# A windowed-attention network in one software pipeline: value products in 16 tiles, two normalizations on GpSimd, and the stages in another order

## The reference, cut to what matters

```python
xn  = layernorm(x) * g1 + b1                      # over the 48 channels
xw  = 7x7 windows of roll(xn, -shift)             # 64 windows of N = 49 tokens per image
q, k, v = split(xw @ qkv_w + qkv_b)               # 6 heads of D = 8 channels
attn = softmax(q*D**-0.5 @ k.T + bias[head] + mask[window])
x  = x + roll(window_reverse((attn @ v) @ proj_w + proj_b), shift)
x  = x + gelu((layernorm(x) * g2 + b2) @ fc1_w + fc1_b) @ fc2_w + fc2_b
```

## Time and profile before

| | |
|---|---|
| median of 3 runs | 5848.9 us (5840.44 to 5856.62) |
| profiled execution | 5841.79 us, its span 5840.0 us |
| busy share of the span | PE 96%, PEld 66%, DVE 83%, ACT 69%, POOL 49% |
| mean granted PE clock | 0.96 of full speed |
| DMA | 11.9% of 16 engines in the queue of the main part |

### The profile page before, as it was taken

How to read it: one execution, slowest core, us unless ns; L and a number is a source line. 1 busy time by engine, 2 the same in 40 slices (tenths; PEclk the granted TensorE clock), 3 DMA queues, 4 the chain that set the end, 5 groups by cost and what they waited for, 6 DMA issues and landing times.

```text
span 5840.0 us, 273732 instructions
## 1 busy us (share of the span) xinstructions
PE 5586.6 (96%) x114818; PEld 3833.3 (66%) x114818; DVE 4841.7 (83%) x7753; ACT 4010.4 (69%) x6155; POOL 2875.1 (49%) x2457
## 2 busy tenths in 40 slices
PE   6799999999999999999999999999999999999987
PEld 3566666666666666666666666666666666666655
DVE  6688888888888888888888788888887888888864
ACT  0277777777777777777777677777776777777760
POOL 4355545555555555554545455555554554455530
PEclk7699999999999999999999999999999999999985
DMA  7311111111111111111111111111111111111118
GB/s 231 97 28 27 30 25 30 28 29 28 28 29 27 30 27 27 30 27 28 30 27 29 26 30 27 29 28 30 27 29 26 29 28 27 28 27 30 28 40 266
DMA packets 288522, 240.35 MB, mean 41 GB/s; under 512 B 43576, under 2 KB 282906, under 8 KB 287002
## 3 DMA queue, kind: packets, MB, share of 16 engines
q1 hardware_dynamic: 246802, 179.90, 11.9%
q0 software_dynamic: 8192, 22.49, 1.2%
q10 hardware_dynamic: 32282, 20.03, 1.1%
HBM read 112.93 MB, written 109.36 MB: 38 GB/s over the span
## 4 chain that ended last, share of the span: by engine, by line
PE 93%; DMA 3%; issue 3%; DVE 1%; ACTq 0%; ACT 0%; SPq 0%; POOL 0%; DVEq 0%
PE pB L1076 10%; PE pS L1100 10%; PE pS L1088 10%; PE pS L1064 9%; PE pA L1110 6%; PE pA L1152 5%; PE pA L1076 5%; PE pB L1052 5%; PE pS L1076 5%; PE pS L1006 4%; PE pS L1037 4%; PE pB L1131 4%; PE pS L1014 3%; PE pA L1014 3%; PE pA L1142 3%
## 5 line engine op out<-in xcount | busy, mean ns | idle before, releaser
L463 POOL TENSOR_TENSOR S<-S,mx 113x588 f32<-113x588 f32 x1536 | 1803.5, 1185 | 1183.0 <-DVE mx L775 1182.8
L449 POOL TENSOR_TENSOR Kbd<-KT,headmask 128x588 f32<-128x588 f32 x768 | 1018.5, 1326 | 1476.1 <-DVE KT L784 1468.7
L762 DVE TENSOR_TENSOR S<-pS,bias 113x588 f32<-113x588 f32 x1536 | 1145.3, 767 | 357.8 <-PE pS L1064 344.6
L775 DVE TENSOR_REDUCE mx<-S 113x12 f32<-113x588 f32 x1536 | 1126.9, 754 | 0.0
L520 ACT ACTIVATE sq<-pS 112x392 f32<-112x392 f32 x768 | 378.4, 493 | 518.5 <-PE pS L1006 518.2
L1076 PE MATMUL pB<-ident,S 113*113 113x113 f32 x4608 | 651.7, 278 | 0.1
L1100 PE MATMUL pS<-E,keyones 113*32 113x392 f32 x4608 | 626.6, 517 | 26.2 <-issue 26.2
L1076 PEld LDWEIGHTS pB<-ident,S 113*113 113x113 f32 x4608 | 519.1, 180 | 196.1 <-issue 196.1
L1088 PE MATMUL pS<-E,V 113*32 113x98 f32 x18432 | 597.3, 249 | 0.0
L1064 PE MATMUL pS<-Kbd,Qt 24*49 24x147 f32 x24576 | 585.8, 294 | 6.9 <-issue 2.9
L1064 PEld LDWEIGHTS pS<-Kbd,Qt 24*49 24x49 f32 x24576 | 372.5, 118 | 307.9 <-issue 266.4
(11 more groups left out here) (133 smaller groups left out, 9329.7 us busy)
## 6 DMA issues: line engine op xcount, KB each, us to landing
xin<-xT SPq DMA_DIRECT2D x384, 98.0 KB, 2.1
xT<-xout SPq DMA_DIRECT2D x384, 98.0 KB, 1.9
xin<-xT SPq DMA_DIRECT2D x384, 73.5 KB, 2.6
xT<-xout SPq DMA_DIRECT2D x384, 73.5 KB, 1.9
xT<-cm POOLq DMA_DIRECT2D x128, 171.5 KB, 4.0
cm<-xT SPq DMA_DIRECT2D x128, 171.5 KB, 3.5
tm<-in_x SPq DMA_DIRECT2D x128, 147.0 KB
out<-tm ACTq DMA_DIRECT2D x128, 147.0 KB
```

The source lines that it names most:

```text
L449: return pool.tensor_tensor(y, x, m, ALU.mult)
L463: pool.tensor_tensor(s, s, m, ALU.subtract).then_inc(sub_done[half][wh], 1)
L762: dve.tensor_tensor(strided(S[:, b, w, 0, 0, 0:1], [[KEYS, 2], [2 * KEYS, 2 * HP], [1, N]]), strided(pS[0:M2, 2 * wh, 0:1], [[512, 2], [N, ...
L775: dve.tensor_reduce(m, s, AX.X, ALU.max).then_inc(mx_done[half][wh], 1)
```

## The change

1. `value`: one product now gives all 48 value columns of one window (both head halves), and the window half chooses the partitions: windows 0 to 3 come out at partitions 0 to 48, windows 4 to 7 at 64 to 112. 4 x 2 x 2 = 16 products in place of 32. `evac_v` reads each window half for itself, so a head half takes two copies of 192 elements in place of one of 384.
2. `normal1` and `normal2` are issued by POOL and not by DVE, with the same operands.
3. The order of the stages on PE, ACT, DVE, POOL and SP, and the homes in PSUM. `add_bias`, `maxima`, `less_maximum` and `exponentials` remain in their four units. `up`, `hidden_c`, `hidden_ab` and `down_ab`, for instance, now work on s4 where they worked on s5.

```diff
-        HOME = dict(ctr1=0, var1=1, qk=1, value=3, attend=0, sums=1, project=2, ctr2=0, var2=2, up=3, upc=2, down=2, turn00=3, turn01=1, turn10=2, turn11=3)
+        HOME = dict(ctr1=3, var1=3, qk=1, value=2, attend=3, sums=2, project=0, ctr2=0, var2=2, up=2, upc=0, down=1, turn00=2, turn01=3, turn10=3, turn11=1)
...
 # value(j), PE
-                for w in range(P):
+                for k in range(J):
                     for i in range(2):
                         r = HI * i
-                        x = strided(xn1[r:r + C, w, 0, 0:1], [[1, N]])
-                        for hh in range(2):
-                            last = mm(to[HI * hh:HI * hh + N, i, HC * w:HC * (w + 1)], x,
-                                      wv[r:r + C, t, HC * hh:HC * (hh + 1)], start=True, stop=True)
+                        for wh in range(2):
+                            x = strided(xn1[r:r + C, J * wh + k, 0, 0:1], [[1, N]])
+                            last = mm(strided(to[HI * wh:HI * wh + N, i, HC * k:HC * k + 1], [[J * HC, 2], [1, HC]]), x,
+                                      wv[r:r + C, t, :].rearrange("p (a n) -> p a n", a=2), start=True, stop=True)
...
 # evac_v(j, hh), DVE
-                src = strided(home("value")[r:r + N, 0, 0:1], [[512, 2], [D, P * HP], [1, D]])
-                dst = strided(V[r:r + N, j.mod(4), 0, 0, o:o + 1], [[2 * D, 2], [VW, P * HP], [1, D]])
-                return dve.tensor_copy(dst, src)
+                for wh in range(2):
+                    at = HI * wh
+                    src = strided(home("value")[at:at + N, 0, J * HC * hh:J * HC * hh + 1], [[512, 2], [D, J * HP], [1, D]])
+                    dst = strided(V[r:r + N, j.mod(4), J * wh, 0, o:o + 1], [[2 * D, 2], [VW, J * HP], [1, D]])
+                    last = dve.tensor_copy(dst, src)
+                return last
...
 # normal1 and normal2: the same bodies, moved from the DVE block to the POOL block
-                dve.wait_ge(rs1_done, gv(j, 1, 1))
+                pool.wait_ge(rs1_done, gv(j, 1, 1))
...
-                dve.tensor_tensor(xn2[:, :], x1[:, j.mod(2)].rearrange("p r c -> p (r c)"), rs2[:, :], ALU.mult)\
+                pool.tensor_tensor(xn2[:, :], x1[:, j.mod(2)].rearrange("p r c -> p (r c)"), rs2[:, :], ALU.mult)\
...
 # SP
-                if s5:
-                    store(s5)
+                if s4:
+                    store(s4)
...
-            LATEST = [(0, 0)]
+            LATEST = [(1, 0)]
```

More of the change, by code:

```diff
@@ L612, in iteration @@
                     inverse_sums(s3)
[L613 to L616, removed]
+                if s4:
+                    hidden_c(s4)
+                if s4:
+                    hidden_ab(s4)
+                    normal_table()
             sweep(act, iteration)
@@ L878, in iteration @@
             def iteration(s0, s1, s2, s3, s4, s5, s6):
+                if s0:
+                    evac_k(s0)
+                if s0:
+                    evac_q(s0)
+                if s0:
+                    evac_va(s0)
+                if s3:
+                    residual1(s3)
+                if s0:
+                    evac_vb(s0)
                 if s4:
-                    normal_o(s4)
+                    residual2(s4)
                 if s1:
-                    evac_k(s1)
+                    maxima(s1, 1, 1)
                 if s1:
-                    evac_q(s1)
-                if s4:
-                    residual1(s4)
-                if s2:
[L888 to L906, removed]
-                if s0:
[L908 to L912, removed]
+                    maxima(s1, 1, 0)
+                if s0:
+                    add_bias(s0, 0, 0)
+                if s0:
+                    add_bias(s0, 0, 1)
+                if s0:
+                    maxima(s0, 0, 0)
+                if s0:
+                    add_bias(s0, 1, 0)
+                if s0:
+                    add_bias(s0, 1, 1)
+                if s2:
+                    normal_o(s2)
+                if s0:
+                    maxima(s0, 0, 1)
             sweep(dve, iteration)
@@ L1243, in iteration @@
                     elif s4:
-                        pe.wait_ge(lo_done, gv(s4, 1, 1))
-                    var1(s0)
-                if s4:
-                    if s2:
-                        pe.wait_ge(bias_done[1][0], gv(s2, 1, 1))
+                        pe.wait_ge(oT_done, gv(s4, 1, 1))
+                    elif s1:
+                        pe.wait_ge(va1_done, gv(s1, 1, 1))
+                    turn_scores(s3, 1, 0)
+                if s4:
+                    if s3:
+                        pe.wait_ge(exp_done[0][0], gv(s3, 1, 1))
+                    elif s1:
+                        pe.wait_ge(v_done, gv(s1, 1, 1))
+                    elif s5:
+                        pe.wait_ge(hAB_done, gv(s5, 1, 1))
+                    elif s4:
+                        pe.wait_ge(lo_done, gv(s4, 1, 1))
+                    var2(s4)
+                if s1:
+                    if s4:
+                        pe.wait_ge(sq2_done, gv(s4, 1, 1))
+                    elif s5:
+                        pe.wait_ge(hC_done, gv(s5, 1, 1))
+                    elif s2:
+                        pe.wait_ge(bias_done[1][0], gv(s2, 1, 1))
+                    if s3:
+                        pe.wait_ge(exp_done[1][1], gv(s3, 1, 1))
+                    elif s5:
+                        pe.wait_ge(x2_done, gv(s5, 1, 1))
+                    elif s1:
+                        pe.wait_ge(q_done, gv(s1, 1, 1))
+                    elif s2:
+                        pe.wait_ge(bias_done[1][1], gv(s2, 1, 1))
+                    ready()
+                    scores(s1, 0)
+                if s0:
+                    if s3:
+                        pe.wait_ge(exp_done[1][0], gv(s3, 1, 1))
                     elif s0:
@@ L1333, in iteration @@
-                if s3:
+                    sums(s3)
+                if s1:
                     if s1:
@@ L1356, in iteration @@
                     elif s1:
-                        pe.wait_ge(bias_done[0][1], gv(s1, 1, 1))
-                    elif s0:
-                        pe.wait_ge(va1_done, gv(s0, 1, 1))
-                    query_key(s0)
+                        pe.wait_ge(v_done, gv(s1, 1, 1))
+                    value(s0)
+                if s3:
+                    if s4:
+                        pe.wait_ge(hC_done, gv(s4, 1, 1))
+                    elif s1:
+                        pe.wait_ge(bias_done[1][0], gv(s1, 1, 1))
+                    project(s3)
+                if s4:
+                    if s0:
+                        pe.wait_ge(q_done, gv(s0, 1, 1))
+                    elif s1:
+                        pe.wait_ge(bias_done[1][1], gv(s1, 1, 1))
+                    elif s3:
+                        pe.wait_ge(exp_done[1][1], gv(s3, 1, 1))
+                    elif s5:
+                        pe.wait_ge(x2_done, gv(s5, 1, 1))
+                    down_ab(s4)
             sweep(pe, iteration)
```

309 lines of the change are left out of this document (126 added, 183 removed).

## The result

The changed kernel takes 5480.1 us in the median of 4 runs (5476.99 to 5482.14), against 5845.5 of before beside it: ratio 0.9372, 95% interval 0.9356 to 0.9388. That is 365 us, twice the forecast gain, and outside the stated range. The profiled execution took 5478.5 us, its span 5476.5.

What follows compares the result with a forecast made beforehand. PE's stages in sequence, 13.59 us per iteration, were taken as the bound. 5841.8 - 77 (iteration) - 63 (stalls) - 40 (slow clock) = 5662, as median 5669 us; own range 5600 to 5720, 8 in 10 5595 to 5800.

Steps and rivals of the forecast that it cites:

- The value products: PE's `value` stage: 16 products of 48 columns in place of 32, 0.35 us less per iteration (0.20 if dearer).
- The order on PE: PE's stages in new order, at the earlier chain's prices: about 0.13 us dearer per iteration.
- The stalls and the clock: PE's issue stalls at `value` and `sums`: 63 of 84 us go; of the slow clock's 78 us, 40 go.
- density: PE stalls where it uses up its instruction list faster than it is brought; spreading dense stages removes 63 us.
- The normalizations on POOL: `normal1` and `normal2` on POOL: 0.8 us for 392 elements, about 1.2 for the shifted `normal1`; hidden, cost 0.
- The copies: DVE's copies of V before the first transpose: 0.35 us each with 192 elements fewer, done 0.2 us early.
- rival 2: A DVE chain up to the first transposes takes PE's place, PE stands 0.4 us per iteration: 5925 us; chance 0.11.

Runs made afterwards that it cites:

- short logarithm: Against the kernel before, `log_sums` takes the logarithm of only the first quarter of the columns from the second step on: 5731.7 us, ratio 0.9834.

## Why the prediction was wrong

- *The value products*: right. Priced at 0.35 less (0.36 + 0.16 = 0.52 in the chain), measured 0.51 in the chain and 0.34 less by the kernel with the old products.
- *The order on PE*: here it failed, and this is the larger part of the miss: 141 of the 185 us by which the forecast gain of 180 fell short (218 - 77 for the iteration; the stalls and the clock gave 140 - 103 = 37 more). The prediction took 0.78 + 0.74 + 0.74 for three transposes in a row, reading 0.74 in the earlier trace rows as what a second transpose costs, and said that "stage follows stage without a wait for another engine". 0.15 of it was a wait for `lo_done` (the run with the short logarithm shows it), which the chain books as the transpose's own time. The own price is 0.59, and the term was taken twice in the new order, where that wait stands in neither place: 0.30. Both `scores` took 0.68 where 0.74 and 0.70 were taken: 0.08 more; why have one at 0.74 was not tested. `down_ab` took 0.67 for 0.65. 13.37 - 0.30 - 0.08 + 0.02 = 13.01, the measured spacing of the chain. So the rest of the change was not a cost of 0.13 but a gain of 0.23 beside the products' 0.34, and the 77 us for both became 218.
- *The stalls and the clock*: right in kind, small in size. 103 us were taken of 181, 140 went of 206. All stalls at `value` and `sums` went, and with them most of the slow clock: from 300 to 5300 us the granted clock was at the lower level for 119 us before and for 34 us after. That the stalls are waits for the list is shown by the packets of q8; that density decides where they come is not shown. It passed two tests (new products: stalls down to 7 us at `value`; moved transfers: unchanged) and failed two (old products in the new order: none; short logarithm: half). The first pass is weaker than it looks, as that kernel also stands for `add_bias` just behind `value`, which gives the list time; a run that tells the two apart is missing. So the 140 us were partly luck: the forecast had the right sign by a rule that does not hold as stated.
- *The range*: with the forecast's 77 us for the iteration, all 206 us of stalls and clock would have given 5566 us. So 5480 was out of reach whatever the stalls did; what the range lacked was a shorter iteration.
- *The normalizations on POOL*: hidden, as said, but dearer: 1018 ns for `normal2` where 0.8 us were taken, and 1010 + 251 + 240 for the shifted `normal1`. The sentence that the trace agrees in size with a factor of two set 2.0 against 1.45 ns per element, a factor of 1.4, and the 2.0 came from an instruction with one operand broadcast; the like comparison is 1018 against 567 ns, a factor of 1.8. The move is also worth something: undoing it costs 31 us in the new order, and in the old one it brings 70 (5727 to 5657), since there it takes away the wait for `normal_o`. POOL's `spread_k` fell from 1326 ns in the mean to 1167, as the prediction had from the earlier trace rows: in the kernel before it took 1490 ns where it ran beside a normalization on DVE (379 times) and 1166 where not. This needed no move to POOL; with the normalizations on DVE in the new order it is 1167 too.
- *The copies* took 355 ns (0.35 taken), and no release before the first transposes was late: rival 2 didn't come.
- *The share of the order and the homes*: with all else equal (13.46 to 13.02, 5657 against 5475 to 5480 us) about 180 us, half of the gain. Without them the rest of the change brings 3%.

## What to carry to other kernels

An engine that is busy 98% of the time (PE from 300 to 5300 us) can still wait in every iteration: where a chain gives the same work two prices (0.74 and 0.59 here), look for the release that ends just before the dearer one, before either is used to price another order. A saving on the bound engine counts only as far as the next release in its order comes early enough; 0.35 us of products were worth 0.13 in one order and 0.34 in another. Relieving another engine counts where one of its releases is the last to come: here 1.83 us less on DVE brought 0.27. And an order packed closer on the bound engine is not better by itself: three that saved about 0.3 of its work lost 0.4 to 0.6 to waits.

## What the runs showed of the hardware that was not expected

- A product on POOL with two SBUF operands of 392 elements took 1018 ns beside 1185 ns for 588 with one operand broadcast; 28 and 21 elements took 251 and 240 ns. The 2.0 ns per element of the 588 is thus not a price that carries over: by it the 392 would take 0.8 us. An estimate from 1018 and 251 ns is 2.1 ns per element and 0.19 us besides.
- A product on DVE with two SBUF operands (112 x 392) took 567 ns in all 384 steps where no instruction of POOL ran beside it (normalizations on DVE, new order), and 1091 ns in the median beside POOL (before). POOL's 128 x 588 product took 1166 ns alone and 1490 beside such a product. The place in the order decides which.
- PE's instruction list came in packets of 256 instructions, and a stalled PE went on 1.2 to 1.7 us after the end of one (107 of 107 stalls of before at `value` and `sums`).
- The stalls of PE named "issue" depend on something that shifted with 0.15 us of timing (84 to 40 us at an unchanged list of PE). Moving the kernel's own loads and stores by 3.6 us or one iteration did nothing.
